# Layer 1 of a two-layer GNN kernel: the running sums over edges, done feature by feature in chunks of 16 tiles

## The chip, the cores and the metric

The kernel runs on one core of a Trainium2 chip, in one launch. The metric is the device time in microseconds (us); the time before is the median of three runs.

## The reference

There are 12500 nodes with 64 features and 200000 edges, sorted by their destination `dst`. Layer 0 is graph attention with 4 heads. Layer 1, the one that is changed, is this:

```python
concat = jnp.concatenate([x[src], x[dst], edge_attr_32], axis=-1)
h = jax.nn.relu(concat @ W1 + b1)                 # 128 wide
messages = h @ W2 + b2
aggregated = segment_sum(messages, dst) / maximum(degree, 1)[:, None]
x = layernorm(x + aggregated + (x @ Wn + bn))
```

W1 has 64 rows for the sender, 64 for the receiver and 32 for the edge. `segment_sum` adds the rows of all edges with the same `dst`.

## The kernel before

**Layout.** The edges are padded to 128 * 1568 and laid out so that each of the 128 partitions (lanes) has 1568 consecutive edges. A tile is one edge of every lane, 128 edges. Since the edges are sorted by destination, the edges of a node are neighbours in a lane. The mask `same` is 1 where an edge has the destination of the one before it, otherwise 0. A sum over the edges of a node is a running sum along the lane, `acc = same * acc + row`, read out at the last edge of the node.

**Before the stage.** Layer 0 has its own chunks of 32 tiles. Its running sums are scans of 32 elements (line 1057), and at its start four scans of 1568 elements spread the destination's attention terms (line 1021). At its end two tables are in device memory: `table1s` with x @ W1[sender], and `table1d` with x @ W1[receiver] + b1. Receiver rows are scattered into `recv_term` at the first edge of each node only, the other rows being zero (`scatter_first`, line 489), so that the same running sum spreads them over the node's edges.

**Layer 1, edge stage.** It goes in chunks of C1 = 8 tiles, 196 of them, each with 8 * 128 features per lane, in rings of four buffers (slot s):
- GpSimd (`gather1`, line 525) issues one indirect DMA per tile, which fetches the 128 sender rows from `table1s` into `G1[s]`. It waits for `relu_done` of the chunk four before, and for the indices `ix1_ready`.
- SyncE (`chunk1`, line 370) loads the edge terms for TensorE, the receiver rows into `X1[s]`, and stores the finished rows from `H1[s]`.
- TensorE (`edge1`, line 682) multiplies the edge terms into two PSUM banks per chunk.
- VectorE (`turn1`, line 1178) does the running sum of the receiver rows of chunk c tile by tile (line 1191), and in turn with it that of the relu rows of chunk c - 1 (line 1197): one instruction of 128 features per tile and kind. Then it waits for the gathers, adds `X1` to `G1` (line 1209) and the PSUM banks (line 1214).
- ScalarE (`turn1`, line 829) applies relu from `G1[s]` to `H1[s]` and copies the indices of a later chunk (line 726).

Each engine takes its instructions in the written order and waits on semaphores; no planner reorders anything. Before the stage VectorE does two adds of 6400 elements (lines 1168 and 1169), one of them through `b2_part` in `node_arena`. Behind the stage GpSimd waits for the stored rows and gathers the last row of each node (`gather_last`, line 484), and W2 is applied to these.

Of the kernel before, what the change touches and what calls it, by code (L numbers as in the profile page):

```python
# [21 lines left out]
P = 128  # L22
# [23 lines left out]
C1 = 8  # L46
# [14 lines left out]
def build(nc, x, xT2, src, dst, e16g, e32g, W_node2, W_nodeT2, attn2, W_edge_bd, W1e_bd, W1n, gamma, beta,  # L61
# [21 lines left out]
    with ExitStack() as ctx:  # L83
# [83 lines left out]
        X1 = [part(edge_arena, (RING1 + s) * W1R, C1, HID) for s in range(RING1)]  # L167
        H1 = [part(edge_arena, (2 * RING1 + s) * W1R, C1, HID) for s in range(RING1)]
# [41 lines left out]
        mc = part(node_arena, 5696, H)  # L210

# [48 lines left out]
        recv_in = [sem(f"recv_in{s}") for s in range(RING1)]  # L260
        e32_in = [sem(f"e32_in{s}") for s in range(RING1)]
        edge1_mm, pre_ready, relu_done = sem("edge1_mm"), sem("pre_ready"), sem("relu_done")
        dv1, rows1_ready, recv_used = sem("dv1"), sem("rows1_ready"), sem("recv_used")
        rows1_stored = [sem(f"rows1_stored{s}") for s in range(RING1)]
# [13 lines left out]
        def _(sp):  # L278
# [82 lines left out]
            for s in range(RING1):  # L361
                sp.dma_start(edge_terms[s][:, 0:2, :], e32g[:, 2 * s:2 * s + 2, :]).then_inc(e32_in[s], 16)
            for r in range(2):
                sp.wait_ge(pds_scattered[r], 16 * (NB // 2 + 1))
            for s in range(RING1 - 1):
                sp.dma_start(X1[s], recv_p[:, s * C1:s * C1 + C1, :]).then_inc(recv_in[s], 16)
            sp.wait_ge(recv_used, 1)
            sp.dma_start(X1[3], recv_p[:, 3 * C1:4 * C1, :]).then_inc(recv_in[3], 16)

            def chunk1(c, s, loads):  # L370
# [12 lines left out]
            for c in range(K1 - RING1, K1):  # L383
                chunk1(c, c % RING1, False)
# [19 lines left out]
        def _(pool):  # L404
# [126 lines left out]
            pool.indirect_dma_start(X1[3][:, C1 - 1, :], None, table1d,  # L531
# [6 lines left out]
            with pool.Fori(0, K1 // RING1 - 1) as it:  # L538
                for slot in range(RING1):
# [5 lines left out]
                    gather1(slot)  # L545


            for s in range(RING1):
                pool.wait_ge(rows1_stored[s], 16 * (K1 // RING1 + 1))
# [13 lines left out]
        def _(pe):  # L563
# [118 lines left out]
            def edge1(c, s, it):  # L682
                pe.wait_ge(e32_in[s], it * 16 + 16)
                pe.wait_ge(pre_ready, c + 1)
                for g in range(2):
                    last = mm(ps[:, 2 * s + g, :], edge_terms[s][:, g, :], w1e_bd[:, :])
                last.then_inc(edge1_mm, 1)

            with pe.Fori(0, K1 // RING1) as it:
                for s in range(RING1):  # L690
                    edge1(it * RING1 + s, s, it)


            pe.wait_ge(rows1_ready, K1 + 1)
            pe.wait_ge(pre_ready, K1 + RING1)
            mm(ps[:, 0, 0:P], H1[(K1 - 1) % RING1][:, C1 - 1, :], same_segT[:, :]).then_inc(carry1_mm, 1)
# [27 lines left out]
        def _(act):  # L724
# [104 lines left out]
            def turn1(c, s, it, copies):  # L829
                act.wait_ge(rows1_stored[s], it * 16 + 16)  # L830
                act.wait_ge(pre_ready, c + (1 + RING1))
                act.activation(H1[s], G1[s], ACT.Relu).then_inc(relu_done, 1)  # L832
                if copies:
                    ix_copy(s, bass.ds(c * C1 + RING1 * C1, C1), C1, ix1_ready)

            with act.Fori(0, K1 // RING1 - 1) as it:
                for s in range(RING1):
                    turn1(it * RING1 + s, s, it, True)
            for c in range(K1 - RING1, K1):
                turn1(c, c % RING1, c // RING1, False)  # L840
# [21 lines left out]
        def _(dve):  # L862
# [14 lines left out]
            dve.sem_inc(pre_ready, RING1)  # L877
# [298 lines left out]
            HOLDS, STEPS1 = C1, 2 * C1 - 1  # L1176

            def turn1(c, s, it, start, first=False, final=False):
                X, Xb = X1[s], X1[(s - 1) % RING1]
                Hc, Hb = H1[(s - 1) % RING1], H1[(s - 2) % RING1]  # L1180
                if not final:
                    dve.wait_ge(recv_in[s], it * 16 + 16)
                if not first:
                    dve.wait_ge(relu_done, c)
                    dve.wait_ge(rows1_ready, c)
                n = 0
                for u in range(C1):
                    if not final:
                        if u:
                            dve.wait_ge(dv1, start + (n - (0 if first else 1)))  # L1190
                        stt(X[:, u, :], X[:, u - 1, :] if u else Xb[:, C1 - 1, :], same[:, bass.ds(c * C1 + u, 1)],  # L1191
                            X[:, u, :], ALU.mult, ALU.add).then_inc(dv1, 1)
                        n += 1
                    if not first:
                        if u:
                            dve.wait_ge(dv1, start + (n - (0 if final else 1)))
# [113 lines left out]
```

## Time and profile before

| | |
|---|---|
| Median of 3 runs | 5625.36 us (5599.26 to 5630.11) |
| Span of the profiled execution | 4755.7 us |
| The profiled execution's own time | not listed beside its span |
| Instructions | 33914 |
| GpSimd (POOL) busy | 75% |
| VectorE (DVE) busy | 55% |
| TensorE busy | 28% |
| ScalarE busy | 10% |
| DMA | 622.28 MB, 131 GB/s over the span |

The span goes from the first to the last instruction of one execution; the time of a run also holds what lies around it. Layer 0's edge stage lies between about 311 and 2265 us, layer 1's between about 2590 and 4597 us. A busy share says how long an engine worked, not whether anything waited for it. An indirect DMA is counted as busy on GpSimd while GpSimd writes its descriptors; the data lands later.

### The profile page before, as it was taken

Reading aid. Unit: us, or ns where it says so; the run is one execution under the profiler, and the core shown is the slowest. Engines: PE = TensorE matmul, PEld = TensorE weight load, DVE = VectorE, ACT = ScalarE, POOL = GpSimd, SP = SyncE. Lnnn points to the kernel's source line nnn. Section 1 sums busy time; section 2 is a strip of 40 time slices with the busy share of each in tenths; the row PEclk is TensorE's granted clock in tenths of the full one; section 3 lists DMA queues with packets and bytes.
Section 4 is the critical chain, followed back from the end, with each engine's and each line's share of the span. In section 5 each row is a group of like instructions: output and inputs, shape, how many; then the busy total and the mean of one; then the engine's idle time right before and its main releaser. Section 6 shows DMA issues by size and latency. Waiting matters only on the chain. (4 is left out here: it accounts for less than half of the span.)

```text
span 4755.7 us, 33914 instructions
## 1 busy us (share of the span) xinstructions
PE 1308.6 (28%) x3363; PEld 660.9 (14%) x3363; DVE 2619.7 (55%) x8568; ACT 493.5 (10%) x1011; POOL 3565.7 (75%) x3558
## 2 busy tenths in 40 slices
PE   7600000000000000000575333333333333333336
PEld 4300000000000000000453111111111111111126
DVE  6545443344433444433774666666666666666645
ACT  4500000000000000000232111111111111111101
POOL 5777777777777777777676777777777777777766
PEclk9855555555555555555555655655665556556655
DMA  3034333333333333333232555555555555555532
GB/s 124 10 112 160 100 105 118 118 117 112 93 118 118 118 118 99 106 118 113 85 121 94 169 171 167 165 170 170 162 170 171 161 170 171 166 166 171 170 104 63
DMA packets 240932, 622.28 MB, mean 131 GB/s; under 512 B 74956, under 2 KB 102543, under 8 KB 221521
## 3 DMA queue, kind: packets, MB, share of 16 engines
q1 hardware_dynamic: 127568, 443.81, 28.2%
q0 software_dynamic: 113280, 177.74, 14.7%
q14 instruction: 78, 0.63, 0.0%
q8 instruction: 6, 0.10, 0.0%
HBM read 328.11 MB, written 293.29 MB: 131 GB/s over the span
## 5 line engine op out<-in xcount | busy, mean ns | idle before, releaser
L525 POOL DMA_INDIRECT edge_arena<-table1s,ix x1568 | 1518.0, 968 | 477.9 <-issue 435.2
L433 POOL DMA_INDIRECT edge_arena<-table,ix x1440 | 1460.5, 1014 | 438.9 <-issue 438.9
L565 PE MATMUL ps<-w1e_bd,edge_terms 128*128 128x512 f32 x784 | 725.1, 1080 | 1264.4 <-DMA edge_terms<-e32g_d 1264.4
L1191 DVE SCALAR_TENSOR_TENSOR edge_arena<-edge_arena,same 128x128 f32<-128x128 f32 x1568 | 542.0, 346 | 263.6 <-issue 189.1
L565 PE MATMUL ps<-we_bd,edge_terms 128*128 128x32 f32 x392 | 93.6, 403 | 1864.1 <-DVE score L1038 1803.8
L1035 DVE TENSOR_TENSOR score<-edge_arena,node_wide 128x128 f32<-128x128 f32 x49 | 14.2, 291 | 1066.0 <-DMA edge_arena<-table,ix 1065.6
L1057 DVE TENSOR_TENSOR_SCAN edge_arena<-wq,edge_arena 128x32 f32<-128x32 f32 x3136 | 586.8, 268 | 1.8
L1197 DVE SCALAR_TENSOR_TENSOR edge_arena<-edge_arena,same 128x128 f32<-128x128 f32 x1568 | 539.7, 344 | 1.5 <-ACT edge_arena L832 1.2
L565 PEld LDWEIGHTS ps<-w1e_bd,edge_terms 128*128 128x128 f32 x784 | 229.0, 322 | 1759.2 <-issue 1759.2
L1209 DVE TENSOR_TENSOR edge_arena<-edge_arena 128x1024 f32<-128x1024 f32 x196 | 240.9, 1229 | 404.5 <-DMA edge_arena<-table1s,ix 404.5
L832 ACT ACTIVATE edge_arena<-edge_arena 128x1024 f32<-128x1024 f32 x196 | 207.0, 1056 | 1800.9 <-DVE edge_arena L1214 1800.9
L565 PEld LDWEIGHTS ps<-we_bd,edge_terms 128*128 128x128 f32 x392 | 87.2, 328 | 1870.5 <-DVE score L1038 1769.3
L484 POOL DMA_INDIRECT node_arena<-rows,end_ix x200 | 210.5, 1053 | 96.5 <-issue 59.4
L1214 DVE TENSOR_TENSOR edge_arena<-edge_arena,ps 128x512 f32<-128x512 f32 x392 | 251.8, 683 | 6.7
L748 ACT ACTIVATE wq<-expo 128x256 f32<-128x256 f32 x49 | 20.4, 416 | 2028.3 <-DVE expo L1049 2028.3
L450 POOL DMA_INDIRECT edge_arena<-table,ix x128 | 143.3, 1120 | 39.0 <-issue 39.0
L489 POOL DMA_INDIRECT recv_term<-node_arena,start_ix x100 | 120.6, 1206 | 48.4 <-issue 32.7
L565 PE MATMUL ps<-node_arena 128*128 128x512 bf16 (+1 forms) x800 | 146.3, 332 | 28.5 <-DVE row_base L953 16.4
L565 PE MATMUL ps<-w1n,node_arena 128*128 128x128 f32 (+1 forms) x400 | 133.9, 488 | 24.1 <-ACT node_arena L777 24.1
L455 POOL DMA_INDIRECT dst_term<-a_dst,start_idx x100 | 104.9, 1049 | 30.5 <-issue 30.5
L742 ACT ACTIVATE node_arena<-ps,node_half 128x1057 bf16<-128x1057 f32 x100 | 114.3, 1143 | 63.4 <-PE ps L565 58.9
L1053 DVE TENSOR_TENSOR edge_arena<-edge_arena,wq 128x2048 f32<-128x2048 f32 x49 | 111.9, 2284 | 0.0
(177 smaller groups left out, 1462.5 us busy)
## 6 DMA issues: line engine op xcount, KB each, us to landing
recv_term<-zeros SPq DMA_DIRECT2D x98, 1024.0 KB, 9.1
edge_arena<-recv_term SPq DMA_DIRECT2D x196, 512.0 KB, 4.1
rows<-edge_arena SPq DMA_DIRECT2D x196, 512.0 KB, 5.1
rows<-edge_arena SPq DMA_DIRECT2D x49, 1152.0 KB, 4.4
edge_arena<-table,ix POOLq DMA_INDIRECT x1568
edge_terms<-e32g_d SPq DMA_DIRECT2D x196, 128.0 KB, 4.8
edge_arena<-table1s,ix POOLq DMA_INDIRECT x1568
edge_terms<-e16g_d SPq DMA_DIRECT2D x49, 256.0 KB, 9.2
```

The source lines that it names most:

```text
L433: pool.indirect_dma_start(G0[slot][:, u, :], None, table0, bass.IndirectOffsetOnAxis(ap=ix[slot][:, u:u + 1], axis=0)).then_inc(gathered0[ ...
L450: pool.indirect_dma_start(G0[slot][:, u, :], None, table0, bass.IndirectOffsetOnAxis(ap=ix[slot][:, u:u + 1], axis=0)).then_inc(gathered0[ ...
L484: pool.indirect_dma_start(RG[r][:, b, :], None, rows, bass.IndirectOffsetOnAxis(ap=end_ix[r][:, b:b + 1], axis=0)).then_inc(done[r], 16)
L489: pool.indirect_dma_start(recv_term, bass.IndirectOffsetOnAxis(ap=start_ix[r][:, b:b + 1], axis=0), PDs[r][:, b, :], None, bounds_check=NE ...
L525: pool.indirect_dma_start(G1[slot][:, u, :], None, table1s, bass.IndirectOffsetOnAxis(ap=ix[slot][:, u:u + 1], axis=0)).then_inc(gathered1 ...
L565: return pe.matmul(out_, lhsT, rhs, start=start, stop=stop)
L832: act.activation(H1[s], G1[s], ACT.Relu).then_inc(relu_done, 1)
L1057: scan(R[:, :, f], wq[:, :, H + f // HD], G[:, :, f], before[:, f:f + 1], ALU.mult, ALU.add)
L1191: stt(X[:, u, :], X[:, u - 1, :] if u else Xb[:, C1 - 1, :], same[:, bass.ds(c * C1 + u, 1)], X[:, u, :], ALU.mult, ALU.add).then_inc(dv1, 1)
L1197: a = stt(Hc[:, u, :], Hc[:, u - 1, :] if u else Hb[:, C1 - 1, :], same[:, bass.ds(c * C1 - C1 + u, 1)], Hc[:, u, :], ALU.mult, ALU.add)
L1209: tt(G1[s], G1[s], X, ALU.add).then_inc(recv_used, 1)
L1214: last = tt(part_g, part_g, ps[:, 2 * s + g, :], ALU.add)
```

## The change

The chunks of layer 1 have 16 tiles (98 chunks). The running sums no longer go tile by tile. ScalarE copies the receiver rows into a buffer in which the 16 edges of one feature lie side by side, with one more column ahead of them for the carry (T1 = 17, 128 * 17 = 2176 elements), and a second such buffer holds the mask, with 0 in the carry column. One `tensor_tensor_scan` over all 2176 elements, with multiply and add, then does the whole chunk: the 0 in each carry column starts the next feature afresh, with the value in that column. The relu rows go the same way: ScalarE writes relu into such a buffer, VectorE scans it, ScalarE turns it back into `H1`. There are four ring buffers for gathered rows as before, one buffer for loaded receiver rows in place of four, and two for the stored rows. These new buffers lie in `node_arena`, and so GpSimd and SyncE wait for `arena_free` before the stage.

```diff
-C1 = 8
+C1 = 16
...
+        T1 = C1 + 1
+        F1 = [part(node_arena, i * HID * T1, HID * T1) for i in range(5)]
+        F1_f = [f.rearrange("p (f t) -> p f t", t=T1) for f in F1]
+        hold1, XF1, HF1 = (0, 1), 2, (3, 4)
+        X1 = part(node_arena, 5 * HID * T1, C1, HID)
+        lead = part(node_arena, 5 * HID * T1 + W1R, HID)
...
+            sp.wait_ge(arena_free, 1)
+            sp.dma_start(X1, recv_p[:, 0:C1, :]).then_inc(recv_in, 16)
+
+            def chunk1(c, s, loads, follows=True):
+                r = s % 2
+                if follows:
+                    sp.wait_ge(xf_ready, c + 1)
+                    sp.dma_start(X1, recv_p[:, bass.ds(c * C1 + C1, C1), :]).then_inc(recv_in, 16)
                 if loads:
                     sp.wait_ge(edge1_mm, c + 1)
-                    sp.dma_start(edge_terms[s][:, 0:2, :], e32g[:, bass.ds(c * 2 + 2 * RING1, 2), :]).then_inc(e32_in[s], 16)
-                    sp.wait_ge(recv_used, c + 2)
-                    sp.dma_start(X1[s], recv_p[:, bass.ds(c * C1 + RING1 * C1, C1), :]).then_inc(recv_in[s], 16)
+                    sp.dma_start(edge_terms[s][:, :, :], e32g[:, bass.ds(c * 4 + 4 * RING1, 4), :]).then_inc(e32_in[s], 16)
                 sp.wait_ge(rows1_ready, c + 2)
-                sp.dma_start(rows1_p[:, bass.ds(c * C1, C1), :], H1[s]).then_inc(rows1_stored[s], 16)
+                sp.dma_start(rows1_p[:, bass.ds(c * C1, C1), :], H1[r]).then_inc(rows1_stored[r], 16)
...
-            pool.indirect_dma_start(X1[3][:, C1 - 1, :], None, table1d,
+            pool.wait_ge(arena_free, 1)
+            pool.indirect_dma_start(lead, None, table1d,
...
                 pe.wait_ge(e32_in[s], it * 16 + 16)
-                pe.wait_ge(pre_ready, c + 1)
-                for g in range(2):
-                    last = mm(ps[:, 2 * s + g, :], edge_terms[s][:, g, :], w1e_bd[:, :])
+                pe.wait_ge(psum1_free, c + 1)
+                for g in range(4):
+                    last = mm(ps[:, 4 * (s % 2) + g, :], edge_terms[s][:, g, :], w1e_bd[:, :])
                 last.then_inc(edge1_mm, 1)
...
-            def turn1(c, s, it, copies):
-                act.wait_ge(rows1_stored[s], it * 16 + 16)
-                act.wait_ge(pre_ready, c + (1 + RING1))
-                act.activation(H1[s], G1[s], ACT.Relu).then_inc(relu_done, 1)
+            def hold_1(c, r):
+                act.activation(F1_f[hold1[r]][:, :, 1:T1], same[:, bass.ds(c * C1, C1)].unsqueeze(1).to_broadcast([P, HID, C1]),
+                               ACT.Copy).then_inc(hold1_ready, 1)
+
+            def recv_1(c):
+                act.wait_ge(recv_in, c * 16 + 16)
+                act.wait_ge(xf_free, c + 1)
+                act.activation(F1_f[XF1][:, :, 1:T1].rearrange("p f t -> p t f"), X1, ACT.Copy).then_inc(xf_ready, 1)
+
+            def turn1(c, s, copies, follows=True, holds=True):
+                r = s % 2
+                act.wait_ge(pre_ready, c + 1)
+                act.wait_ge(rows1_ready, c + 1)
+                act.activation(F1_f[HF1[r]][:, :, 1:T1].rearrange("p f t -> p t f"), G1[s], ACT.Relu).then_inc(relu_done, 1)
                 if copies:
                     ix_copy(s, bass.ds(c * C1 + RING1 * C1, C1), C1, ix1_ready)
-
+                if follows:
+                    recv_1(c + 1)
+                act.wait_ge(scanned1, c + 2)
+                act.wait_ge(rows1_stored[r], (c - r) * 8 + 16)
+                act.activation(H1[r], F1_f[HF1[r]][:, :, 1:T1].rearrange("p f t -> p t f"), ACT.Copy).then_inc(rows1_ready, 1)
+                if holds:
+                    hold_1(c + 2, r)
...
-            link(dve.memset(H1[RING1 - 1][:, C1 - 1, :], 0.0))
+            dve.memset(F1_f[hold1[0]][:, :, 0:1], 0.0)
+            link(dve.memset(F1_f[hold1[1]][:, :, 0:1], 0.0))
             dve.sem_inc(rows1_ready, 1)
+            dve.sem_inc(scanned1, 1)
+            dve.sem_inc(arena_free, 1)
             dve.wait_ge(lane_recv_in, 16)
...
+            by_edge = lambda i: F1_f[i][:, :, 1:T1].rearrange("p f t -> p t f")
+
+            def sums1(c, r, turn):
+                dve.wait_ge(dv1, turn * STEPS_1 + 1)
+                dve.wait_ge(relu_done, c + 1)
+                scan(F1[HF1[r]], F1[hold1[r]], F1[HF1[r]], 0.0, ALU.mult, ALU.add).then_inc(scanned1, 1)
+
+            def lead1(c, r):
+                dve.wait_ge(scanned1, c + 1)
+                dve.wait_ge(rows1_ready, c + 1)
+                dve.tensor_copy(F1_f[HF1[r]][:, :, 0:1], F1_f[HF1[1 - r]][:, :, C1:T1]).then_inc(dv1, 1)
+
+            def turn1(c, s, it, first=False):
+                r = s % 2
+                if first:
+                    dve.sem_inc(dv1, 1)
+                else:
+                    lead1(c - 1, 1 - r)
+                dve.wait_ge(gathered1[s], it * (16 * C1) + 16 * C1)
+                dve.wait_ge(edge1_mm, c + 1)
+                pre = G1[s].rearrange("p t f -> p (t f)")
+                tt(pre, pre, ps[:, 4 * r:4 * r + 4, :].rearrange("p a b -> p (a b)"), ALU.add).then_inc(psum1_free, 1)
...
+                    sums1(c - 1, 1 - r, c)
+                dve.wait_ge(xf_ready, c + 1)
+                dve.wait_ge(hold1_ready, c + 1)
+                dve.wait_ge(xf_free, c + 1)
+                scan(F1[XF1], F1[hold1[r]], F1[XF1], 0.0, ALU.mult, ALU.add).then_inc(dv1, 1)
...
+                dve.wait_ge(dv1, c * STEPS_1 + 2)
+                dve.wait_ge(psum1_free, c + 3)
+                tt(G1[s], G1[s], by_edge(XF1), ALU.add).then_inc(pre_ready, 1)
+                dve.tensor_copy(F1_f[XF1][:, :, 0:1], F1_f[XF1][:, :, C1:T1]).then_inc(dv1, 1)
+                dve.wait_ge(pre_ready, c + 1)
+                dve.wait_ge(dv1, c * STEPS_1 + 3)
+                dve.sem_inc(xf_free, 1)
+                dve.sem_inc(dv1, 1)
```

## Rows read from the trace of the kernel before

**Rows 1.** Span; then busy time, share and instructions by engine.

```profile
span 4755.7 us, 33914 instructions
...
PE 1308.6 (28%) x3363; PEld 660.9 (14%) x3363; DVE 2619.7 (55%) x8568; ACT 493.5 (10%) x1011; POOL 3565.7 (75%) x3558
```

**Rows 2.** Costliest groups: out<-in, count | busy us, mean ns | idle before.

```profile
L525 POOL DMA_INDIRECT edge_arena<-table1s,ix x1568 | 1518.0, 968 | 477.9 <-issue 435.2
...
L1191 DVE SCALAR_TENSOR_TENSOR edge_arena<-edge_arena,same 128x128 f32<-128x128 f32 x1568 | 542.0, 346 | 263.6 <-issue 189.1
...
L1209 DVE TENSOR_TENSOR edge_arena<-edge_arena 128x1024 f32<-128x1024 f32 x196 | 240.9, 1229 | 404.5 <-DMA edge_arena<-table1s,ix 404.5
L832 ACT ACTIVATE edge_arena<-edge_arena 128x1024 f32<-128x1024 f32 x196 | 207.0, 1056 | 1800.9 <-DVE edge_arena L1214 1800.9
...
L1214 DVE TENSOR_TENSOR edge_arena<-edge_arena,ps 128x512 f32<-128x512 f32 x392 | 251.8, 683 | 6.7
```

**Rows 3.** Window of the stage, busy us; last: granted clock, DMA, GB/s.

```profile
2600.00:4560.00 1960.00, 716.32 (x768) 225.40 (x768) 1317.02 (x3667) 222.79 (x385) 1489.72 (x1544) 0.57 0.55 168
```

**Rows 4.** GpSimd's waits in that window: total us, times, longest us.

```profile
POOL edge_arena L525 <- ACT edge_arena L832: 42.1, 138, 0.3
```

**Rows 5.** GpSimd's timeline (start us, us) behind the stage; first, twentieth gather.

```profile
4597.49 0.94 POOL L484 DMA_INDIRECT node_arena<-rows,end_ix  x1 [11.97 <-DMA rows<-edge_arena]
...
4621.20 0.94 POOL L484 DMA_INDIRECT node_arena<-rows,end_ix  x1 [0.30 <-issue]
```

**Rows 6.** Timeline beside four long scans; the first two of four gathers.

```profile
299.83 13.61 DVE L1021 TENSOR_TENSOR_SCAN node_wide<-same,lane_rows,node_wide 128x1568 f32<-128x1568 f32 x4 [76.48 <-DMA node_wide<-dst_term]
...
300.22 3.85 POOL L450 DMA_INDIRECT edge_arena<-table,ix  x1 [0.30 <-issue]
304.37 3.07 POOL L450 DMA_INDIRECT edge_arena<-table,ix  x1 [0.30 <-issue]
```

**Rows 7.** Timeline ahead of the stage: two adds of 6400, scatters, lead row.

```profile
2564.80 6.85 DVE L1168 TENSOR_TENSOR node_arena<-has,row_bc 128x6400 f32<-128x6400 f32 x1 [19.00 <-DMA table1s<-node_arena]
2571.68 6.82 DVE L1169 TENSOR_TENSOR node_wide<-node_wide,node_arena 128x6400 f32<-128x6400 f32 x1
2578.60 0.17 DVE L1172 MEMSET edge_arena<- 128x128 f32 x1
...
2566.07 6.43 POOL L489 DMA_INDIRECT recv_term<-node_arena,start_ix  x1 [0.30 <-issue]
2572.80 6.56 POOL L489 DMA_INDIRECT recv_term<-node_arena,start_ix  x1 [0.30 <-issue]
...
2588.59 0.98 POOL L531 DMA_INDIRECT edge_arena<-table1d,ends_i  x1 [0.31 <-issue]
```

**Rows 8.** Layer 0: scans of 32 (group); a product of 2048, its gather.

```profile
L1057 DVE TENSOR_TENSOR_SCAN edge_arena<-wq,edge_arena 128x32 f32<-128x32 f32 x3136 | 586.8, 268 | 1.8
...
616.65 2.28 DVE L1053 TENSOR_TENSOR edge_arena<-edge_arena,wq 128x2048 f32<-128x2048 f32 x1
...
617.01 2.73 POOL L433 DMA_INDIRECT edge_arena<-table,ix  x1 [0.30 <-issue]
```

**Rows 9.** Timeline of a chunk's landing: two gathers, and VectorE's adds.

```profile
4575.29 0.94 POOL L525 DMA_INDIRECT edge_arena<-table1s,ix  x1 [0.30 <-issue]
4575.38 1.23 DVE L1209 TENSOR_TENSOR edge_arena<-edge_arena 128x1024 f32<-128x1024 f32 x1 [3.71 <-DMA edge_arena<-table1s,ix]
4576.54 0.94 POOL L525 DMA_INDIRECT edge_arena<-table1s,ix  x1 [0.30 <-issue]
4576.64 1.28 DVE L1214 TENSOR_TENSOR edge_arena<-edge_arena,ps 128x512 f32<-128x512 f32 x2
```

**Rows 10.** Stage's end: last landing, last store; a ScalarE group of 512.

```profile
4587.18 1.23 DVE L1209 TENSOR_TENSOR edge_arena<-edge_arena 128x1024 f32<-128x1024 f32 x1 [3.73 <-DMA edge_arena<-table1s,ix]
...
4594.00 0.33 SPq L378 DMA_DIRECT2D rows<-edge_arena  x1
...
L847 ACT ACTIVATE node_arena<-ps 128x512 f32<-128x512 f32 x20 | 11.9, 597 | 117.8 <-PE ps L706 117.8
```

More of the change, by code:

```diff
@@ L166, in build @@
         G1 = [part(edge_arena, s * W1R, C1, HID) for s in range(RING1)]
-        X1 = [part(edge_arena, (RING1 + s) * W1R, C1, HID) for s in range(RING1)]
-        H1 = [part(edge_arena, (2 * RING1 + s) * W1R, C1, HID) for s in range(RING1)]
+        H1 = [part(edge_arena, (RING1 + r) * W1R, C1, HID) for r in range(2)]
         score = sb("score", [P, C0, H])
@@ L259, in build @@
         gathered1 = [sem(f"gathered1_{s}") for s in range(RING1)]
-        recv_in = [sem(f"recv_in{s}") for s in range(RING1)]
+        recv_in, xf_ready, xf_free = sem("recv_in"), sem("xf_ready"), sem("xf_free")
+        hold1_ready, scanned1, psum1_free, arena_free = sem("hold1_ready"), sem("scanned1"), sem("psum1_free"), sem("arena_free")
         e32_in = [sem(f"e32_in{s}") for s in range(RING1)]
         edge1_mm, pre_ready, relu_done = sem("edge1_mm"), sem("pre_ready"), sem("relu_done")
-        dv1, rows1_ready, recv_used = sem("dv1"), sem("rows1_ready"), sem("recv_used")
-        rows1_stored = [sem(f"rows1_stored{s}") for s in range(RING1)]
+        dv1, rows1_ready = sem("dv1"), sem("rows1_ready")
+        rows1_stored = [sem(f"rows1_stored{r}") for r in range(2)]
         carry1_mm, carry1_cp = sem("carry1_mm"), sem("carry1_cp")
@@ L382, in _ @@
                     chunk1(it * RING1 + s, s, True)
-            for c in range(K1 - RING1, K1):
-                chunk1(c, c % RING1, False)
+            for c in range(K1 // RING1 * RING1 - RING1, K1):
+                chunk1(c, c % RING1, c + RING1 < K1, c + 1 < K1)
             def store_out(k, r):
@@ L545, in _ @@
                     gather1(slot)
-            for s in range(RING1):
-                pool.wait_ge(rows1_stored[s], 16 * (K1 // RING1 + 1))
+            for c in range(K1 // RING1 * RING1, K1):
+                pool.wait_ge(ix1_ready, c + 1)
+                pool.wait_ge(relu_done, c - RING1 + 1)
+                gather1(c % RING1)
+            for r in range(2):
+                pool.wait_ge(rows1_stored[r], 16 * (K1 // 2 + 1))
             for r in range(2):
@@ L691, in _ @@
                     edge1(it * RING1 + s, s, it)
+            for c in range(K1 // RING1 * RING1, K1):
+                edge1(c, c % RING1, c // RING1)
             pe.wait_ge(rows1_ready, K1 + 1)
[L695 to L696 removed]
+            pe.wait_ge(psum1_free, K1 + 2)
+            mm(ps[:, 0, 0:P], H1[(K1 - 1) % 2][:, C1 - 1, :], same_segT[:, :]).then_inc(carry1_mm, 1)
             pe.wait_ge(carry1_cp, 1)
@@ L1217, in _ @@
-            turn1(0, 0, 0, 0, first=True)
-            with dve.Fori(0, K1 // RING1 - 1) as it:
-                for i in range(RING1):
-                    c = it * RING1 + (i + 1)
-                    turn1(c, (i + 1) % RING1, it + (i + 1) // RING1, it * (RING1 * STEPS1) + (HOLDS + i * STEPS1))
-            for c in range(K1 - RING1 + 1, K1):
-                turn1(c, c % RING1, c // RING1, HOLDS + (c - 1) * STEPS1)
-            turn1(K1, K1 % RING1, K1 // RING1, HOLDS + (K1 - 1) * STEPS1, final=True)
+            dve.tensor_copy(F1_f[XF1][:, :, 0:1], lead.unsqueeze(2)).then_inc(xf_free, 1)
@@ L1226, in _ @@
+            turn1(0, 0, 0, first=True)
+            with dve.Fori(0, K1 // RING1) as it:
+                for i in range(RING1):
+                    turn1(it * RING1 + (i + 1), (i + 1) % RING1, it + (i + 1) // RING1)
+            turn1(K1 - 1, (K1 - 1) % RING1, (K1 - 1) // RING1)
+            lead1(K1 - 1, (K1 - 1) % 2)
+            sums1(K1 - 1, (K1 - 1) % 2, K1)
             dve.wait_ge(rg0_in[0], 16 * NB // 2)
@@ L1231, in _ @@
             dve.wait_ge(carry1_mm, 1)
+            for r in range(2):
+                dve.wait_ge(rows1_stored[r], 16 * (K1 // 2 + 1))
             dve.tensor_copy(rgT[0][:, 0:P], ps[:, 0, 0:P]).then_inc(carry1_cp, 1)
```

60 lines of the change are left out of this document (12 added, 48 removed).

## The prediction, made before the changed kernel had run

> **What bounds the kernel now.** I read the busy shares first, then the costliest groups, then the windows and the waits, and last the timeline at the few places where VectorE runs something long. GpSimd is the busiest engine [rows 1], and in layer 1 it does one thing: 1568 indirect gathers, one per tile of 128 edges, 968 ns each with 0.30 us of "issue" between them [rows 2]. Between 2600 and 4560 us it issues 1544 of them in 1960 us, 1.2694 us each [rows 3]. Its longest wait for ScalarE's relu there is 0.3 us, the same 0.3 that it has between any two gathers [rows 4], so the ring of gather buffers never holds it back. VectorE is busy 1317 of the 1960 us (67%), ScalarE 223 (11%) [rows 3]: neither sets the end. The stage lasts as long as GpSimd's gathers. Where VectorE is quiet, after the last chunk, 19 gathers take 4621.20 - 4597.49 = 23.71 us, 1.248 each [rows 5]. So the 0.34 us steps of today's running sums cost GpSimd only 1.2694 - 1.248 = 0.021 us per gather.
>
> What matters for this change is what a **long** VectorE instruction does to a gather. Three places show it. Beside the four scans of 1568 elements, back to back for 13.61 us, GpSimd gets through exactly one gather per scan, of 3.85 and then about 3.07 us, in place of 0.94 [rows 6]. Beside the two adds of 6400 elements the indirect scatters take 6.43 and 6.56 us, and the first of them ends at 2572.50, 0.85 us after the add that it met ended at 2571.65 [rows 7]. Beside the product of 2048 elements a gather takes 2.73 us [rows 8]. So a gather needs something at about 0.12 us of its life (0.97 - 0.85) that a VectorE instruction with two SBUF operands holds until its end; it is let in between two such instructions, ends 0.82 us later, and asks again after 0.30 + 0.12: one period, 1.248 us. The add out of PSUM doesn't do this: a gather that starts 0.10 us ahead of it, at 4576.54, takes its 0.94 [rows 9].
>
> The Trainium skill says of this (SBUF — State Buffer, "Who interferes with whom") that a VectorE instruction with two SBUF inputs contends with GpSimd instructions that read SBUF, but infers that tensor_tensor leaves descriptor generation alone, since that would need the write side only. By that inference nothing would be added here, and the sum would be that of rival A below. The trace disagrees, with 6.43 us for 0.97 [rows 7].
>
> As a formula: for n such instructions back to back over W us, GpSimd loses W - U - (n - 1) * 1.248, where U, between 0 and 1.248, is the time from the start of the first to the next moment at which a gather asks. It reproduces the rows: 13.61 - 0.51 - 3 * 1.248 = 9.4 against (3.85 + 3 * 3.07) - 4 * 0.94 = 9.3 [rows 6]; W = 2578.50 - 2564.80 = 13.70, U = 2566.19 - 2564.80 = 1.39 (the scatter that began with the add was past the point), 13.70 - 1.39 - 1.25 = 11.1 against 6.43 + 6.56 - 2 * 0.97 = 11.1 [rows 7].
>
> **The change, part by part.**
> *Gathers.* 1568 as before, issued in the same order; none is taken away. A buffer now holds 16 tiles and there are still four, so GpSimd may run 64 tiles ahead instead of 32. No wait goes, since none was there [rows 4].
>
> *VectorE, removed.* Per 16 tiles 32 steps of 346 ns that started 0.26 us apart and two adds of 1229 ns [rows 2]. With them goes what they cost GpSimd: 1568 * 0.021 = 34 us.
>
> *VectorE, added, per chunk of 16 tiles.* Two scans over 128 features of 17 = 2176 elements. A scan costs (3461 - 268) / (1568 - 32) = 2.08 ns per element beyond 268 ns for 32 (3461: 13.61 us for four that overlap by 0.08 [rows 6]; 268 is in [rows 8]), so 268 + 2144 * 2.08 = 4.73 us. One add of 2048 from SBUF: 2.28, as measured at that size [rows 8]. One add out of PSUM of 2048: from 1024 to 2048 elements the SBUF adds rise by 2.28 - 1.23 = 1.05 us [rows 2, 8], so 683 ns for 512 [rows 2] become 0.68 + 1.5 * 1.05 = 2.26 us. Two column copies of 128 elements, nearest row the 0.17 us memset of 128 [rows 7], and up to 0.3. In all some 14.5 us, against 19.96 us that GpSimd needs alone: VectorE has time enough. But the order decides: gathered wait, PSUM add (holds nothing), scan of the relu rows, scan of the receiver rows, SBUF add. Nothing that these wait for is late (relu of the chunk before came after the turn before; the receiver rows were turned a chunk ahead), so the three holding instructions stand back to back: W = 4.73 + 4.73 + 2.28 = 11.7 us, n = 3.
> U: today's first instruction behind the landing starts 0.09 us after a gather's start [rows 9]; the first scan starts 2.18 us (2.26 less the 0.08 by which the scans overlap) later, at 2.27; the second gather from there starts at 2.50 and asks at 2.62, so U = 0.3. It can lie anywhere from 0 to 1.25, so the loss is 8.0 to 9.2 per chunk, and I take 11.7 - 0.3 - 2.5 = 8.9. It falls in 97 of the 98 chunks, since behind the last gather nothing is held: 97 * 8.9 = 863 us (773 to 894). The column copies I take at nothing; if they hold too, at most 0.5 per chunk, 49 us.
>
> *ScalarE, added.* Four passes of 2048 per chunk (mask, receiver rows in, relu in, rows out). 1056 ns for 1024 and 597 for 512 [rows 2, 10] give 0.9 ns per element, 1.97 us a pass, 8 us a chunk, beside GpSimd's 29: hidden. Queued behind its wait for scanned1 are the rows out, the mask and the next relu; the next relu isn't wanted before the next chunk has landed. Its strided passes aren't in the trace: at twice the price they make 14 us, still hidden, and 6 us more at the very end.
>
> *Transfers and waits.* The same bytes in transfers twice as large; the receiver rows have one buffer, loaded as soon as ScalarE has turned the last ones, a whole chunk ahead. SP waits for xf_ready before it refills the edge terms, which are four chunks ahead. TensorE's four matmuls per chunk instead of twice two wait for a bank pair that VectorE frees right at the start of its turn; it is busy 37% [rows 3]. All hidden. The new wait of GpSimd for arena_free at the start of the stage stands before every gather. VectorE gives it behind the adds, where the memset now is, at 2578.6, and GpSimd is busy with its last scatters until it issues the lead row at 2588.59 [rows 7]: 10 us of cover, so nothing. Without the cover it would be up to the 13.7 us of the two adds.
>
> *The end of the stage.* Behind the last landing VectorE starts at 4587.18 [rows 10] and the first gather of the last stage goes out at 4597.49 [rows 5]: 10.3 us. Afterwards: PSUM add 2.2, scan 4.7, scan 4.8, add 2.3, relu 2.05, the last scan of sums 4.8, rows out 2.05, and the store, 3.5 us for 512 KB now (4594.00 to 4597.49), 3.5 to 7 for twice that, say 5. Sum 27.9, so 18 us more.
>
> **Sum.** -34 + 863 + 18 = +847 us. The profiled span of 4755.7 becomes about 5603. The three times shown have a median of 5625.36, 870 us over the span; what lies around the span isn't itemized, the change touches none of it, and I keep it: 5625 + 847 = **6472 us**, 15% slower. VectorE's own busy time falls a little, and it isn't what counts.
>
> **Rivals.**
> *A. Nothing is held.* If the hold were a matter of those early places and not of this stage (today's 0.34 us steps, which also have two SBUF operands, cost only 0.02 us per gather), GpSimd would run at 1.248 throughout: -34 + 18 = -16, 5609 us, which is not slower. Against it: short instructions leave a gap every 0.2 to 0.3 us, so they show the same rule, and rows 6 are scans of this very form. Chance 0.06. It decides from the point where W - U - (n - 1) * 1.248 is zero, that is where no instruction with two SBUF operands is longer than a period.
> *B. The strided operand is slow.* The SBUF add reads the receiver rows 17 words apart, and no row has an add like that. At a scan's pace, 2.08 ns per element, it would take 0.15 + 2048 * 0.00208 = 4.4 us, and the 2.1 more are held: 97 * 2.1 = 206, in all 6678 us. For it: ScalarE's passes share the stride. Against: the scans of 32 elements step over whole rows of 72 words, and their 268 ns leave room for no price beyond 2.08 ns per element [rows 8]. Chance 0.11. The Trainium skill (Advanced Engine Details and Errata, "SBUF Cachelines") speaks for it: accesses that each fall on another 16-byte line pay. It names no price, and no run here shows it.
> *C. No gather is let in between.* If a waiting gather lost the race at both seams, the loss would be 11.7 - 0.3 = 11.4 per chunk, 97 * 11.4 = 1106, 6715 us. Against it are the four gathers of rows 6. Chance 0.03.
>
> **How the numbers follow.** My own case has 0.80; its range is 6380 to 6505. The range given reaches up to B and a little below: 6365 to 6690. A measurement of this kernel tells 0.5%, some 28 us, from no change. Slower holds my case, B and C: 0.94. A straddles "same" (5609): same 0.04, faster 0.02.
>
> **What would show it.** In the changed trace: gathers in the stage at about 0.94 us except for three per chunk, of some 4.5 to 5.5, 4.4 and 2 us; period of a chunk about 28.9 us (19.96 + 8.9) instead of 20.3; scans at 4.7 us each; VectorE's wait ahead of the PSUM add for gathers, some 14 us per chunk; GpSimd never idle for relu_done. The SBUF add at 2.3 us refutes B, at over 3 it makes the time B's. I am wrong if the gathers beside the scans take 0.94 us (A), or if the wait in front of the PSUM add is gone, because then another engine bounds the stage.

## The result, and the profile after

The changed kernel took 6083.78 us (median of 4 runs, 6079.43 to 6088.13), the kernel before 5627.73 us beside it: 1.083 times the time, interval 1.079 to 1.086, so 8% slower. The forecast was 6472, 15% slower, with a range of 6365 to 6690. The direction was right, the size was outside.

The page of the changed kernel, from its profiled execution (its own time 6088.13 us); in the groups the columns are those of [rows 2]:

```profile
span 6086.0 us, 23598 instructions
...
PE 1178.8 (19%) x3343; PEld 653.7 (11%) x3363; DVE 2935.5 (48%) x5435; ACT 1570.3 (26%) x1109; POOL 4508.5 (74%) x3558
...
L531 POOL DMA_INDIRECT edge_arena<-table1s,ix x1568 | 2483.5, 1584 | 477.8 <-issue 477.8
L439 POOL DMA_INDIRECT edge_arena<-table,ix x1440 | 1444.4, 1003 | 625.0 <-issue 433.1
L1091 DVE TENSOR_TENSOR_SCAN edge_arena<-wq,edge_arena 128x32 f32<-128x32 f32 x3136 | 684.7, 276 | 875.4 <-issue 856.4
...
L862 ACT ACTIVATE edge_arena<-node_arena 128x2048 f32<-128x2048 f32 x98 | 387.9, 3958 | 1394.4 <-DVE node_arena L1220 1394.4
...
L1220 DVE TENSOR_TENSOR_SCAN node_arena<-node_arena 128x2176 f32<-128x2176 f32 x98 | 459.0, 4684 | 3.2 <-ACT node_arena L855 3.2
L1242 DVE TENSOR_TENSOR_SCAN node_arena<-node_arena 128x2176 f32<-128x2176 f32 x98 | 457.3, 4666 | 0.0
L855 ACT ACTIVATE node_arena<-edge_arena 128x2048 f32<-128x2048 f32 x98 | 375.1, 3828 | 285.6 <-DVE edge_arena L1247 285.6
L849 ACT ACTIVATE node_arena<-node_arena 128x2048 f32<-128x2048 f32 x98 | 373.9, 3815 | 16.2 <-DMA node_arena<-recv_term 14.1
L1247 DVE TENSOR_TENSOR edge_arena<-edge_arena,node_arena 128x2048 f32<-128x2048 f32 x98 | 370.8, 3783 | 11.8
...
L843 ACT ACTIVATE node_arena<-same 128x2048 f32 (+1 forms) x98 | 193.8, 1979 | 15.4 <-DVEq L1210 15.4
```

Three readings ("issue" is time in which an engine waited for nothing that the profile shows). The mean gather went from 968 [rows 2] to 1584 ns, with the same 0.30 us between gathers: the gather stage takes 2483.5 + 477.8 = 2961 us, where [rows 2] give 1518.0 + 477.9 = 1996. The scans last 4.68 us, as forecast, but the SBUF add lasts 3.78 and not 2.28. And this span is the execution's own time but for 2 us, while the span in [rows 1] lies 870 us under the runs of its kernel; layer 0's scans, which the change doesn't touch, now have 856 us of "issue" ahead of them, and had 1.8 us of idle time [rows 8].

One chunk of the changed kernel on GpSimd and on VectorE (timeline; start us, us):

```profile
3997.29 0.95 POOL L531 DMA_INDIRECT edge_arena<-table1s,ix  x1 [0.30 <-issue]
3998.54 0.94 POOL L531 DMA_INDIRECT edge_arena<-table1s,ix  x1 [0.30 <-issue]
3999.79 5.22 POOL L531 DMA_INDIRECT edge_arena<-table1s,ix  x1 [0.30 <-issue]
4005.32 4.28 POOL L531 DMA_INDIRECT edge_arena<-table1s,ix  x1 [0.30 <-issue]
4009.90 3.67 POOL L531 DMA_INDIRECT edge_arena<-table1s,ix  x1 [0.31 <-issue]
4013.88 0.94 POOL L531 DMA_INDIRECT edge_arena<-table1s,ix  x1 [0.30 <-issue]
...
3997.37 2.29 DVE L1236 TENSOR_TENSOR edge_arena<-edge_arena,ps 128x2048 f32<-128x2048 f32 x1 [14.01 <-DMA edge_arena<-table1s,ix]
3999.58 4.68 DVE L1220 TENSOR_TENSOR_SCAN node_arena<-node_arena 128x2176 f32<-128x2176 f32 x1
4004.18 4.67 DVE L1242 TENSOR_TENSOR_SCAN node_arena<-node_arena 128x2176 f32<-128x2176 f32 x1
4008.96 3.79 DVE L1247 TENSOR_TENSOR edge_arena<-edge_arena,node_arena 128x2048 f32<-128x2048 f32 x1
```

Three long gathers, one per instruction with two SBUF operands, then thirteen of 0.94. The first ends at 3999.79 + 5.22 = 4005.01, 0.83 us behind the start of the next scan (4004.18), and the third 0.82 us behind the end of the add (4012.75). The two gathers beside the 2.29 us add out of PSUM keep their 0.94, and so do those from 4013.88 on, though ScalarE has a strided pass of 3.83 us from 4012.78. U is 3999.91 - 3999.58 = 0.33 us, with the first long gather asking 0.12 us after its start. The two gathers beside the scans are as forecast; the third, beside the add, was forecast at 2 us and takes 3.67.

### The profile page after: what moved, and what is told of

It reads as the page before. It is cut to its first block, busy times and chain, and to the rows that moved or that the text cites. A ratio compares the mean times of both kernels' runs of the same rounds, so it can differ in the third digit from the quotient of the medians.

```text
span 6086.0 us, 23598 instructions
## 1 busy us (share of the span) xinstructions
PE 1178.8 (19%) x3343; PEld 653.7 (11%) x3363; DVE 2935.5 (48%) x5435; ACT 1570.3 (26%) x1109; POOL 4508.5 (74%) x3558
## 4 chain that ended last, share of the span: by engine, by line
POOL 40%; issue 28%; DVE 14%; another core or an unknown queue 11%; PE 5%; ACT 1%; DMA 1%; SPq 0%; DVEq 0%; POOLq 0%; ACTq 0%
POOL edge_arena L531 39%; DVE edge_arena L1091 9%; PE ps L576 5%; DVE edge_arena L1087 1%; ACT node_arena L755 1%; DVE edge_arena L1093 1%; DVE edge_arena L1078 0%; DVE score L1074 0%; DVE score L1072 0%; PE ps L656 0%; DMA node_wide<-dst_term 0%; DVE expo L1081 0%; DVE score L1069 0%; DVE node_wide L1055 0%
## 5 line engine op out<-in xcount | busy, mean ns | idle before, releaser
L531 POOL DMA_INDIRECT edge_arena<-table1s,ix x1568 | 2483.5, 1584 | 477.8 <-issue 477.8
L1091 DVE TENSOR_TENSOR_SCAN edge_arena<-wq,edge_arena 128x32 f32<-128x32 f32 x3136 | 684.7, 276 | 875.4 <-issue 856.4
L576 PE MATMUL ps<-w1e_bd,edge_terms 128*128 128x512 f32 x784 | 577.6, 905 | 2359.0 <-issue 1685.3
L1236 DVE TENSOR_TENSOR edge_arena<-edge_arena,ps 128x2048 f32<-128x2048 f32 x98 | 224.2, 2288 | 1378.4 <-DMA edge_arena<-table1s,ix 1378.4
L862 ACT ACTIVATE edge_arena<-node_arena 128x2048 f32<-128x2048 f32 x98 | 387.9, 3958 | 1394.4 <-DVE node_arena L1220 1394.4
L1220 DVE TENSOR_TENSOR_SCAN node_arena<-node_arena 128x2176 f32<-128x2176 f32 x98 | 459.0, 4684 | 3.2 <-ACT node_arena L855 3.2
L1242 DVE TENSOR_TENSOR_SCAN node_arena<-node_arena 128x2176 f32<-128x2176 f32 x98 | 457.3, 4666 | 0.0
L855 ACT ACTIVATE node_arena<-edge_arena 128x2048 f32<-128x2048 f32 x98 | 375.1, 3828 | 285.6 <-DVE edge_arena L1247 285.6
L849 ACT ACTIVATE node_arena<-node_arena 128x2048 f32<-128x2048 f32 x98 | 373.9, 3815 | 16.2 <-DMA node_arena<-recv_term 14.1
L1247 DVE TENSOR_TENSOR edge_arena<-edge_arena,node_arena 128x2048 f32<-128x2048 f32 x98 | 370.8, 3783 | 11.8
L843 ACT ACTIVATE node_arena<-same 128x2048 f32 (+1 forms) x98 | 193.8, 1979 | 15.4 <-DVEq L1210 15.4
```

Of the source, the lines that this page charges most:

```text
L531: pool.indirect_dma_start(G1[slot][:, u, :], None, table1s, bass.IndirectOffsetOnAxis(ap=ix[slot][:, u:u + 1], axis=0)).then_inc(gathered1 ...
L576: return pe.matmul(out_, lhsT, rhs, start=start, stop=stop)
L849: act.activation(F1_f[XF1][:, :, 1:T1].rearrange("p f t -> p t f"), X1, ACT.Copy).then_inc(xf_ready, 1)
L855: act.activation(F1_f[HF1[r]][:, :, 1:T1].rearrange("p f t -> p t f"), G1[s], ACT.Relu).then_inc(relu_done, 1)
L862: act.activation(H1[r], F1_f[HF1[r]][:, :, 1:T1].rearrange("p f t -> p t f"), ACT.Copy).then_inc(rows1_ready, 1)
L1091: scan(R[:, :, f], wq[:, :, H + f // HD], G[:, :, f], before[:, f:f + 1], ALU.mult, ALU.add)
```

## The experiments

The theory after the result had two parts. First, the hold costs what the formula says, with 3.78 us for the add. Second, the 870 us beside the old span were never around it: that profile was of an execution without a stall that the runs of the first series had. The stall is time in which VectorE's next instruction comes late, though nothing that the profile shows holds it. The rival of the first part was a loss by the total time of VectorE, that of the second a constant time around the span.

The cuts of code below are shortened: where an instruction is cut into pieces, the semaphore increment stands on the last piece, and step counts that go with an edit are left out.

**again: the kernel before, unchanged.**

```diff
 (no edit)
```

> The kernel before, unchanged, once more with a profile. In the changed kernel's profile the span (6086 us) is its own time but for 2 us; the profile of before that the prediction used has a span 870 us under the median of its runs. Theory 1: that profile was of an execution free of a stall that ordinary runs have. In layer 0 of the changed kernel's trace the scans of 32 elements come 0.7 or 1.4 us apart for long stretches (856 us of 'issue' ahead of them), in code that the change doesn't touch, and layer 0 is some 365 us longer than in the old profile. Then a new profile of before has a span of 5600 to 5650, with layer 0 some 350 us longer and layer 1 some 450 to 520 us longer than in the old one, with 'issue' ahead of the tile by tile sums. Theory 2: 870 us lie around the span of this kernel and not of the other: the new profile has a span near 4756 again and a time near 5628.

Measured 5648.97 us beside 5655.20; the span of its profile is 5637.2. Layer 1's first gather comes 306 us later than in the old profile (some 350 expected) and its gather stage is 545 us longer (450 to 520 expected). The groups:

```profile
L525 POOL DMA_INDIRECT edge_arena<-table1s,ix x1568 | 1580.3, 1008 | 960.5 <-ACT ix L726 493.1
...
L1057 DVE TENSOR_TENSOR_SCAN edge_arena<-wq,edge_arena 128x32 f32<-128x32 f32 x3136 | 682.3, 278 | 882.2 <-issue 862.1
L1191 DVE SCALAR_TENSOR_TENSOR edge_arena<-edge_arena,same 128x128 f32<-128x128 f32 x1568 | 547.4, 349 | 713.7 <-issue 595.4
L1197 DVE SCALAR_TENSOR_TENSOR edge_arena<-edge_arena,same 128x128 f32<-128x128 f32 x1568 | 545.4, 348 | 425.0 <-issue 392.2
```

The same kernel as in [rows 2], and another picture: GpSimd waits 493 us for the indices that ScalarE copies behind the relu, since VectorE's tile by tile steps have 988 us of "issue" ahead of them (189 in the trace of [rows 2]), and the gather stage takes 1580.3 + 960.5 = 2541 us instead of 1996. So in this execution it was not the gathers alone that set the pace of layer 1, but VectorE's late steps too. Both traces of this kernel move the same 622.28 MB in the same 240932 packets. Theory 2 of this run is out: nothing of size lies around the span.

**pieces: each scan in four instructions, the SBUF add in four.**

```diff
-scan(F1[i], F1[hold1[r]], F1[i], 0.0, ALU.mult, ALU.add)
+w = HID * T1 // 4
+for k in range(4):
+    f = F1[i][:, k * w:k * w + w]
+    scan(f, F1[hold1[r]][:, k * w:k * w + w], f, 0.0, ALU.mult, ALU.add)
...
-tt(G1[s], G1[s], by_edge(XF1), ALU.add)
+for k in range(4):
+    e = slice(4 * k, 4 * k + 4)
+    tt(G1[s][:, e, :], G1[s][:, e, :], by_edge(XF1)[:, e, :], ALU.add)
```

> The changed kernel with each scan of 2176 elements cut into four of 544 (32 features each) and the SBUF add into four of 4 tiles. Same work and result. Theory of the hold (a gather is shut out until the end of a VectorE instruction with two SBUF operands, and let in between two): pieces of 1.40 and about 1.06 us are no longer than a gather's period of 1.25, so nearly nothing is lost, 0 to 1.5 us per chunk in place of 10.2. Layer 1 at 1.25 to 1.35 us per gather, 840 to 970 us less than the changed kernel: 5110 to 5240 us, below the kernel before as well. Rival (the loss is VectorE's total time with two SBUF operands, however cut, or ScalarE's strided passes): within 100 us of 6084.

5308.74 us beside 5655.20, 0.938 (0.934 to 0.942): 775 us less than the changed kernel, for the same work, and less than the kernel before in that series. The expected 5110 to 5240 was too low. Its timeline says why (scans from 4022.51, 1.23 us apart; add pieces from 4032.55, 0.97 apart; a seam is the point between two pieces):

```profile
4023.49 1.06 POOL L531 DMA_INDIRECT edge_arena<-table1s,ix  x1 [0.30 <-issue]
4024.86 0.94 POOL L531 DMA_INDIRECT edge_arena<-table1s,ix  x1 [0.30 <-issue]
...
4033.61 1.81 POOL L531 DMA_INDIRECT edge_arena<-table1s,ix  x1 [0.30 <-issue]
4035.72 1.64 POOL L531 DMA_INDIRECT edge_arena<-table1s,ix  x1 [0.30 <-issue]
...
4022.51 9.91 DVE L1223 TENSOR_TENSOR_SCAN node_arena<-node_arena 128x544 f32<-128x544 f32 x8
4032.55 3.98 DVE L1258 TENSOR_TENSOR edge_arena<-edge_arena,node_arena 128x512 f32<-128x512 f32 x4
```

Eight scans of 1.31 us go by with gathers of 0.94: the pieces have the gathers' own period, so each gather asks at a seam. Beside the add it asks within a piece and waits for its end.

**unstrided: the SBUF add reads contiguous zeros** (the receiver part is left out of the sum).

```diff
-tt(G1[s], G1[s], by_edge(XF1), ALU.add)
+tt(pre, pre, zeros[:, 0:C1 * HID], ALU.add)
```

> The changed kernel, but the SBUF add of a chunk reads 2048 contiguous zeros in place of the receiver rows 17 words apart (the receiver part is left out of the sum; all else stays). If the 3.78 us of that add are its stride, it takes 2.28 us and each of 97 chunks loses 1.5 us less: 146 us less, 5938 us. If something else makes it slow (its place behind the scans, the hold itself), it stays at 3.8 and the time at 6084.

5931.80 us beside 5655.20, 1.048 (1.042 to 1.053): 152 us less than the changed kernel, 146 expected.

```profile
L531 POOL DMA_INDIRECT edge_arena<-table1s,ix x1568 | 2335.3, 1489 | 477.8 <-issue 477.8
...
L1247 DVE TENSOR_TENSOR edge_arena<-edge_arena,zeros 128x2048 f32<-128x2048 f32 x98 | 224.7, 2292 | 11.8
```

The add falls from 3783 to 2292 ns, at the same place behind the scans, and the gather stage by 148 us, 1.5 per chunk. The stride is the price, and the hold passes it on one to one. (The edit changes the buffer that is read as well as the stride; ScalarE's strided and unstrided passes, below, differ in the same way.)

**The later series.** From here on, in four series, the kernel before took 4752 to 4760 us instead of 5628 to 5655, so each run is read against the kernel before beside it only, or against after2. These series lack the stall, and absolute times expected for the first condition can't be compared with them.

**halves: each scan in two, the add whole.**

```diff
-scan(F1[i], F1[hold1[r]], F1[i], 0.0, ALU.mult, ALU.add)
+w = HID * T1 // 2
+for k in range(2):
+    f = F1[i][:, k * w:k * w + w]
+    scan(f, F1[hold1[r]][:, k * w:k * w + w], f, 0.0, ALU.mult, ALU.add)
```

> The changed kernel with each scan cut into two of 1088 elements; the SBUF add stays whole. A test of the count in the formula W - U - (n - 1) * 1.248: W stays near 13.2 us, n goes from 3 to 5, so a chunk loses 13.2 - 0.3 - 5.0 = 7.9 us in place of 10.3, and 97 * 2.3 = 225 us go: 5860 us. If a gather were let in by chance only, or the loss went by the total time of these instructions, the time would stay within 50 us of 6084.

5511.13 us beside 4754.28, 1.159 (1.157 to 1.161). Against after2, 5738.62, that is 227 us less; 225 expected. The loss per chunk is 16 * ((2249.0 + 477.8) / 1568 - 1.248) = 7.9 us, the forecast number. Timeline:

```profile
3002.99 3.09 POOL L531 DMA_INDIRECT edge_arena<-table1s,ix  x1 [0.30 <-issue]
3006.38 2.01 POOL L531 DMA_INDIRECT edge_arena<-table1s,ix  x1 [0.30 <-issue]
3008.70 2.01 POOL L531 DMA_INDIRECT edge_arena<-table1s,ix  x1 [0.30 <-issue]
3011.01 2.01 POOL L531 DMA_INDIRECT edge_arena<-table1s,ix  x1 [0.30 <-issue]
3013.33 3.67 POOL L531 DMA_INDIRECT edge_arena<-table1s,ix  x1 [0.30 <-issue]
```

Five instructions with two SBUF operands, five long gathers: the count n is what the formula says.

**adds3 and adds3b: as pieces, with the add in three pieces of 5, 5 and 6 tiles.**

```diff
-for k in range(4):
-    e = slice(4 * k, 4 * k + 4)
+for k in range(3):
+    e = slice(k * 16 // 3, (k + 1) * 16 // 3)
```

> As the run with pieces (four per scan), but the SBUF add in three pieces of 5, 5 and 6 tiles in place of four of 4. In the trace of pieces the gathers beside the scans take 0.94 us, since a piece lasts as long as a gather's period and the gathers ask at the seams; those beside the add, whose pieces are 0.98 us apart, take 1.8 and 1.6 us, some 1.6 of the 2.4 us that a chunk still loses. Pieces 1.2 us apart would bring those gathers to the seams too: up to 150 us less, 5150 to 5230 us. If the gathers then ask just behind a seam, each waits for a whole piece more, and it is up to 100 us more than 5309.

> The run adds3 again (scans in four pieces, the SBUF add in three). Where the kernel before takes 4754 it took 4828. Where it takes 5640, its time should be that of pieces there, 5309, less the 1.3 us per chunk that the gathers beside the add no longer lose: 5309 - 97 * 1.4 = 5170, 8% less than before.

4828.35 us beside 4754.28, 1.0155 (1.0138 to 1.0172), and again 4831.34 beside 4759.68, 1.0154. Its gather stage takes 1570.5 + 477.8 = 2048 us, where that of pieces took 1707.6 + 477.9 = 2186: 137 us less, 1.4 per chunk. So 5738.62 (after2) - 4831.34 = 907 of the 980 us that the change costs without the stall are given back. The 5170 us expected under the conditions of the first series were not tested, since no later run met them. Without the stall, then, the best of the cuts is still 1.5% slower than the kernel before; that pieces came out 6% faster in its series goes with the stall of the kernel beside it (without the stall its time would be some 4828 + 137 = 4965 us, an estimate, against 4754).

**after2: the changed kernel again.**

```diff
 (no edit)
```

> The changed kernel once more, beside the kernel before on the same chip. In the last series the kernel before took 4754 us (7 runs), in the ones before it 5628 to 5655: there are two conditions of the chip, with and without late instructions, and the profile that the prediction used is of the one without. Without late instructions the changed kernel takes 4754 + 961 (the gather stage of the run extra, 2957 us, against 1996) + some 20 = 5735 us, 1.206 times the time before, near the ratio that the prediction's terms give with the strided add in them. With late instructions it takes 6085 against 5640, 1.08. One condition for both kernels alike, each a constant offset, would instead give the same difference of about 450 us in both.

5738.62 us beside 4758.95, 1.206 (1.204 to 1.208). Its trace, and the first and last rows of its stage's end:

```profile
span 5735.9 us, 23598 instructions
...
L531 POOL DMA_INDIRECT edge_arena<-table1s,ix x1568 | 2477.4, 1580 | 477.8 <-issue 477.8
L1091 DVE TENSOR_TENSOR_SCAN edge_arena<-wq,edge_arena 128x32 f32<-128x32 f32 x3136 | 586.7, 267 | 1.8
...
5547.38 2.29 DVE L1236 TENSOR_TENSOR edge_arena<-edge_arena,ps 128x2048 f32<-128x2048 f32 x1 [13.98 <-DMA edge_arena<-table1s,ix]
...
5579.82 0.94 POOL L490 DMA_INDIRECT node_arena<-rows,end_ix  x1 [34.08 <-DMA rows<-edge_arena]
```

Here layer 0's scans follow one another without a gap, as in [rows 8], and the sum against the old profile closes: the gather stage 2955 - 1996 = 959 us, its end 32.4 - 10.3 = 22, together 981; the spans differ by 5735.9 - 4755.7 = 980.

**extra: 32 memsets of one column more per turn of VectorE.**

```diff
+pad = sb("pad", [P, 32])
...
 dve.sem_inc(dv1, 1)
+for k in range(32):
+    dve.memset(pad[:, k:k + 1], 0.0)
```

> The changed kernel with 32 memsets of one column added to every turn of VectorE in layer 1, behind its last copy, where it waits 14 us per chunk for gathers. Theory of late instructions (in ordinary runs VectorE's instructions come 0.7 or 1.4 us apart after a short burst, whatever they do): 32 of them take some 20 us or more, which is longer than the gap, and the time rises by 300 to 1000 us, with 'issue' ahead of the memsets. Rival (the stall of layer 0 and of the kernel before belongs to what those instructions do or wait for): 32 * 0.06 = 2 us, hidden, within 30 us of 6084.

> The run extra again (32 memsets more per turn). Where the kernel before takes 4754, they come 0.03 us apart and are hidden: the time of after2 within 15 us, as it was found. Where it takes 5640, the theory of late instructions says that they come up to 0.7 or 1.4 us apart, 10 to 45 us per chunk against 13 us of idle: 100 to 1000 us over after2. Rival: the lateness belongs to what layer 0's instructions do: within 15 us of after2 there too.

> The run extra once more, for the condition with late instructions. Theory (lateness costs by the number of VectorE's instructions): 100 to 1000 us over 6084 where the kernel before takes 5640. Rival (it belongs to what the other instructions do): 6084 within 30. Where before takes 4754: 5740 again.

Four series gave 5740.69, 5736.87, 5742.26 and 5745.01 us, within 7 us of after2. The 32 memsets take 0.93 us in all where VectorE idles 13:

```profile
3018.09 0.93 DVE L1255 MEMSET pad<- 128x1 f32 x32 [0.29 <-DVEq L1253]
```

So without the stall their number costs nothing. None of the four met the conditions of the first series, in which they were meant to decide.

**one_sum: the kernel before without the receiver rows' running sums in layer 1.**

```diff
-stt(X[:, u, :], X[:, u - 1, :] if u else Xb[:, C1 - 1, :], same[:, bass.ds(c * C1 + u, 1)],
-    X[:, u, :], ALU.mult, ALU.add).then_inc(dv1, 1)
-n += 1
```

> The kernel before with the running sum of the receiver rows left out of layer 1 (half of the tile by tile instructions; the receiver rows are then added only at each node's first edge). In its new profile layer 1's gathers take 2541 us, 493 of them waiting for the relu, against 1996 in the first one. If the reason is that VectorE's many instructions come late, half of them is few enough for the gathers to set the pace again: 1.25 to 1.35 us per gather, 420 to 580 us less than 5650, so 5070 to 5230 us. If the late time belongs to something else than their number, the time stays above 5450.

> The run one_sum again (the kernel before without the receiver rows' running sums in layer 1). Where the kernel before takes 4754, it took 4726: the gathers set the pace, and half of VectorE's steps is worth 28 us. Where it takes 5640, the theory of late instructions gives 420 to 580 us less, 5070 to 5230 us, since VectorE then keeps up again; the rival gives 28 us less there too.

> The run one_sum once more, for that condition. Theory: 5070 to 5230 us where the kernel before takes 5640. Rival: some 5610. Where before takes 4754: 4726 again.

4725.95, 4726.34, 4726.75 and 4732.11 us, 0.993 to 0.995 of the kernel beside it (intervals within 0.992 to 0.997): half of the short steps is worth 26 to 33 us. The forecast put all of them at 34, so that term was small. For the first series this run too says nothing.

## Why the prediction was wrong

**The bound, right for the profile it was read from.** GpSimd's gathers set layer 1 in [rows 2] and in the changed kernel; there VectorE waits 14 us per chunk for them, as forecast, and GpSimd never waits for relu_done. Under the conditions in which the two kernels were timed this was not so for the kernel before: by the trace of again, GpSimd waited 493 us for ScalarE behind VectorE's late steps.

**The hold, right.** Forecast 8.9 us per chunk, with the add at 2.28; with the add at its true 3.78 us the formula gives W = 4.60 + 4.78 + 3.79 = 13.2 and 13.2 - 0.3 - 2.5 = 10.4. Measured 16 * (2961 / 1568 - 1.248) = 10.2. It rests on halves (count), pieces (seams) and unstrided (length), not on the one number. Rival A, nothing held, is out; so is C, since one gather went through at each seam. The inference of the Trainium skill (SBUF — State Buffer, "Who interferes with whom") that tensor_tensor leaves descriptor generation alone doesn't hold for these gathers: 3.67 us for 0.94 beside the add. But these gathers also read their indices `ix` from SBUF, and the rule of the same section that the prediction gives, on GpSimd instructions that read SBUF, agrees with the traces. Whether the indices or the descriptors are what is held, no run here separates.

**The strided add, wrong in size.** I took 2.28 us and gave rival B 0.11; it is what happened, at 3.78 instead of its 4.4. It is worth 1.5 us per chunk, 148 us of the stage. The argument against B failed twice over. The price turned out at (3783 - 2292) / 2048 = 0.73 ns per element, and 32 elements would make 23 ns of that in 268, too little to read. And a scan needs 2.08 ns per element anyway; what a faster instruction pays may hide in that, which no run shows by itself. ScalarE's strided passes showed a price too, 3.82 to 3.96 us against 1.98 for the mask, which reads and writes in runs; they stayed hidden, as forecast, except for 4 us at the end. The rule of the Trainium skill (Advanced Engine Details and Errata, "SBUF Cachelines") is that accesses which each fall on another line pay; the add agrees, with 3.78 us against 2.29.

**The end of the stage, nearly.** 18 us forecast, 22 measured.

**The base, wrong, and this is the step that failed.** I wrote that "what lies around the span isn't itemized, the change touches none of it, and I keep it". The 870 us weren't around the span (that is 2 us). They were inside the executions of the first series, as time in which engines waited for their next instruction, and the change took away the part of it that lay in layer 1. A piece of layer 0 in the changed kernel's first trace:

```profile
1009.13 0.29 DVE L1091 TENSOR_TENSOR_SCAN edge_arena<-wq,edge_arena 128x32 f32<-128x32 f32 x1 [1.11 <-issue]
1010.53 0.29 DVE L1091 TENSOR_TENSOR_SCAN edge_arena<-wq,edge_arena 128x32 f32<-128x32 f32 x1 [1.11 <-issue]
1011.93 0.29 DVE L1091 TENSOR_TENSOR_SCAN edge_arena<-wq,edge_arena 128x32 f32<-128x32 f32 x1 [1.11 <-issue]
```

The first gather of layer 1, in the kernel before without and with the stall (before, again) and in the changed kernel without and with it (after2, after):

```profile
2589.88 0.96 POOL L525 DMA_INDIRECT edge_arena<-table1s,ix  x1 [0.30 <-issue]
...
2895.91 0.96 POOL L525 DMA_INDIRECT edge_arena<-table1s,ix  x1 [0.30 <-issue]
...
2590.86 0.96 POOL L531 DMA_INDIRECT edge_arena<-table1s,ix  x1 [0.30 <-issue]
...
2916.96 0.96 POOL L531 DMA_INDIRECT edge_arena<-table1s,ix  x1 [0.30 <-issue]
```

| Stall by the traces, us | ahead of that gather | in the gather stage | behind | in all |
|---|---|---|---|---|
| Kernel before | 306 | 545 | 31 | 5637.2 - 4755.7 = 882 |
| Changed kernel | 326 | 6 | 18 | 6086.0 - 5735.9 = 350 |

In layer 1 the changed kernel has few VectorE instructions and 14 us per chunk to spare, so what comes late there is covered. The 3136 tile by tile steps of before had no such cover. So the change costs 980 us without the stall and 449 with it (6086.0 - 5637.2), and the forecast of +847 stands between. It misses the first by 133 us: 148 for the strided add and 4 at the stage's end, less some 20 by which the other terms were too high. It misses the second by 398 us, because the change also takes away 532 us of stall (539 less in the gather stage, 7 more outside it), which the forecast held fixed. In the absolute time, the base of 5625 us carries 870 us of stall where the changed kernel has 350. That is 520 too much, and the terms were 133 too low: together 387 too high, against 388 measured (6472 - 6084). That the forecast came as near as it did is in part luck, since the two errors have opposite signs.

What makes instructions late in the first series is open. The traces show when they come, not what held them, and that the lateness goes by the number of short instructions is argued from the two traces of that series, not shown: extra and one_sum were to show it and only met the other condition. It isn't a matter of the chip alone: the same chip (number 11) gave 5655 us for the kernel before in the series of again and 4752 in that of the third extra.

## What to carry to other kernels

Where GpSimd issues indirect DMAs and sets the pace, the length of a VectorE instruction with two SBUF operands counted here, not VectorE's busy time: many short ones leave seams, and few long ones shut the gathers out, so cut them to about a gather's period (1.25 us here). When a profiled span and the runs' median differ by 15%, ask first whether the profile shows the execution that was timed: the difference may be a stall inside it, on which the change acts. An operand that no row shows strided has no price yet, and a slower kind of instruction with strided operands (a scan, at 2.1 ns per element) is no evidence for a faster one (an add, at 1.1).

## What the runs showed of the hardware

- A gather meeting a VectorE instruction with two SBUF operands ends 0.8 us behind that instruction's end: 5.22, 4.28 and 3.67 us for 0.94. The 2.29 us add out of PSUM holds nothing, nor does ScalarE's pass of 3.83 us.
- With pieces of 1.31 us that start 1.23 us apart, eight gathers in a row took 0.94 to 1.06 us: nearly no loss, though VectorE was busy without a break.
- An add of 2048 elements with one operand 17 words apart takes 3.78 us on VectorE, contiguous 2.29; a copy or relu of 2048 with that stride takes 3.82 to 3.96 us on ScalarE, 1.98 in runs of 16. Scans show next to none: 3.46 us for 1568 elements 4 words apart [rows 6], where those in sequence take 2.40 us for 1088 (halves) and 4.68 for 2176, that is 3.41 between them.
- The same kernel took 5628 to 5655 us in two series and 4752 to 4760 in four later ones. In the former VectorE's instructions came 0.7 and 1.4 us apart over long stretches.
